# One block for projections, softmax and products of a triangular attention, in place of two

## Chip, cores, metric

One NeuronCore of a Trainium2 chip. The metric is the device time of one execution in microseconds (us); of several executions the median counts. [...]

## What is computed

The program computes two layers over x (2, 64, 64, 256). Only the first is touched by the change, and of it the attention:

```python
B, N, _, E = x_in.shape          # 2, 64, 64, 256
H = 8;  d_k = E // H             # 8 heads of 32
q, k, v1, v2 = (x_in @ W).reshape(B, N, N, H, d_k)   # W = Wq, Wk, Wv1, Wv2
scores = einsum('bilhd,bljhd->biljh', q, k) / sqrt(d_k)
att = softmax(scores, axis=2)    # over l
out = einsum('biljh,bilhd,bljhd->bijhd', att, v1, v2)
attn_out = out.reshape(B, N, N, E) @ Wo
```

Behind it come a residual, two layer norms and an MLP (`block_mlp`), and the second layer, a pair of Mamba scans (`block_mamba`). Neither is changed.

## The kernel before

The program is written out per engine: every engine has its own list of instructions in order, and semaphores (`wait_ge`, `then_inc`) tie the lists together. No scheduler decides an order. A DMA is issued in order by the queue of the engine on whose list it stands: nearly all by SP, some by POOL (GpSimd). PE is the matrix engine (TensorE), DVE VectorE, ACT ScalarE.

`block_projections` takes the 8192 tokens in 16 steps of 512 (`CHUNK`). Each step turns its x on PE (8 transposes), ACT copies the result out as `xT_hi` and DVE subtracts to make `xT_lo` (products use three terms of high and low parts, `SPLIT`), then come 24 matmuls for queries and keys (L208) and 24 for the two values (L218). ACT and DVE copy the results out (L273, L277), POOL's queue stores them to DRAM (`qk_dram` L179, `v_dram` L182).

`block_attention` starts when that block is over. Heads are taken in four pairs (`PAIRS`), n; the two batches stand beside each other. For one pair the work is:

- `scores(n, g)`, 16 groups g of 4 values of l: PE, out of `q` and a chunk `kb` of keys (8 values of l a chunk, two buffers, 4 DMAs a chunk, L359); `copy_scores` by ACT (L545) into `raw`.
- the softmax in 8 parts k of 8 values of j: `least` of the negated scores by DVE (L450), `exps` by ACT (16 instructions a part, each followed by the read of its accumulator, which is the row's sum, L555), `invert` by DVE (L455), `norm` by POOL (L434), `turn(n, g)` by PE (L506, two groups a part), `copy_att` into `att` (L459 by DVE, L562 by ACT).
- the products, 64 steps t of two rows i each: `av` = `att` times v2, 22 of 32 values of d by DVE and 10 by POOL (both L420), then for each row four small groups of matmuls with `w` (v1 spread out, `build` by ACT) on PE (`row`, L520), and `evict` by ACT (L592). `av` has two buffers (a product waits until the rows of the step before last are done), the results three PSUM banks. A store of 4 rows is 8 DMAs on SP's queue (L377).

A stage c is one pair and one batch, 32 steps; there are 8. Its v2 is loaded as `v2in` (values of d next to each other), and ACT turns it (`turn_v2`, 4 instructions, L569 and L573): DVE's part into PSUM, `v2ps`, POOL's into SBUF, `v2sb`. Both products of the stage's first step wait for that. It is done behind row 61 (`i == N - 3`) of the stage before:

```python
if c + 1 < NC and i == N - 3:
    turn_v2(c + 1)
```

For pair 0 scores and softmax stand by themselves, ahead of the first product. For pairs 1 to 3 they are strewn between the 64 product steps of the pair before: scores in steps 0 to 15, exps from step 18 on (`EXPS`), and the rest behind them by the tables `LEAST_AT`, `INVERT_AT`, `NORM_AT`, `TURN_AT`.

Of the kernel before, what the change touches and what calls it, by code (L numbers as in the profile page):

```python
# [112 lines left out]
def block_projections(nc, x, W, qk_dram, v_dram):  # L113

    STEPS = TOK // CHUNK
    with ExitStack() as ctx:
        t_ = Tools(nc, ctx, "prj")  # L120
        sb, sem = t_.sb, t_.sem
        bank = t_.banks()
        T_, Q_, V_ = bank[0:2], bank[2:6], bank[6:8]
        ident = sb("ident", [P, P])
        wqk = sb("wqk", [P, 2, KT, E])
        wv = sb("wv", [P, KT, 2, E])
        wqk_ = {n: sb(f"wqk_{n}", [P, 2, KT, E], F32R) for n in ("hi", "lo")}
        wv_ = {n: sb(f"wv_{n}", [P, KT, 2 * E], F32R) for n in ("hi", "lo")}
        xin = [sb(f"xin{u}", [P, TT, E]) for u in range(2)]
        xT = {n: [sb(f"xT{u}_{n}", [P, KT, CHUNK], F32R) for u in range(2)] for n in ("hi", "lo")}  # L130
        w_split = sem("w_split")
        qk = [sb(f"qk{u}", [P, 4, CHUNK]) for u in range(2)]
        vs = [sb(f"vs{u}", [P, TT, 2 * E]) for u in range(2)]
        ident_set, qk_w_loaded, v_w_loaded = sem("ident_set"), sem("qk_w_loaded"), sem("v_w_loaded")
        x_loaded = [sem(f"x_loaded{u}") for u in range(2)]
        transposed, xT_hi_ready, xT_lo_ready = sem("transposed"), sem("xT_hi_ready"), sem("xT_lo_ready")
        qk_done, qk_by_act, qk_by_dve = sem("qk_done"), sem("qk_by_act"), sem("qk_by_dve")
        v_done, v_by_act, v_by_dve = sem("v_done"), sem("v_by_act"), sem("v_by_dve")
        qk_stored = [sem(f"qk_stored{u}") for u in range(2)]
        v_stored = [sem(f"v_stored{u}") for u in range(2)]  # L140
        block = ctx.enter_context(nc.Block())
        rows = x.rearrange("(g t p) c -> g p t c", t=TT, p=P)
        qk_out = qk_dram.rearrange("(m p) t -> p m t", p=P)
        v_out = v_dram.rearrange("(g t p) c -> g p t c", t=TT, p=P)

        def stages(eng, step):

            step(0, 0, False)
            step(1, 1, False)
            with eng.Fori(1, STEPS // 2 - 1) as r:  # L150
                step(r * 2, 0, False)
                step(r * 2 + 1, 1, False)
            step(STEPS - 2, 0, False)
            step(STEPS - 1, 1, True)

        @block.sync
        def _(sp):
            def load(t, u):
                need(sp, transposed, 2 * t - 2)
                sp.dma_start(xin[u][:, :, :], rows[t]).then_inc(x_loaded[u], 16)  # L160

            load(0, 0)
            for m, name in enumerate(("Wq", "Wk")):
                sp.dma_start(wqk[:, m], W[name].rearrange("(k p) n -> p k n", p=P)).then_inc(qk_w_loaded, 16)
            load(1, 1)
            for m, name in enumerate(("Wv1", "Wv2")):
                sp.dma_start(wv[:, :, m], W[name].rearrange("(k p) n -> p k n", p=P)).then_inc(v_w_loaded, 16)
            with sp.Fori(1, STEPS // 2) as r:
                load(r * 2, 0)
                load(r * 2 + 1, 1)  # L170

        @block.gpsimd
        def _(pool):
            make_identity(pool, ident, ident_set)

            def store(t, u, last):
                pool.wait_ge(qk_by_act, 2 * t + 2)
                pool.wait_ge(qk_by_dve, 2 * t + 2)
                pool.dma_start(qk_out[:, :, bass.ds(t * CHUNK, CHUNK)], qk[u][:, :, :]).then_inc(qk_stored[u], 16)  # L179
                pool.wait_ge(v_by_act, 2 * t + 2)  # L180
# [1590 lines left out]
```

## Time and profile before

| | us |
|---|---|
| median of 3 executions (2548.08 to 2550.58) | 2548.24 |
| the profiled execution | 2545.53 |
| its span, first to last instruction | 2543.9 |
| projections, until the last matmul | 201 |
| scores and softmax of pair 0, until the first product | 109 |
| 256 product steps, until the next block | 868 |
| the two other blocks | 1365 |
| busy: PE 2121, DVE 1982, ACT 1340, POOL 1014 | |

The profile is of one execution on the one core. Busy time of an engine says little here, since the stages have different limits: read each stage by itself, and in it the wait that ends last. `SPq` and `POOLq` are rows of DMAs being issued, not of their transfers. Two instructions that follow each other overlap by some 0.1 us in the rows, so the distance of two starts is the price of one, not its length.

### The profile page before, as it was taken

How to read it: one execution, taken by the hardware profiler on the slowest of the kernel's cores; microseconds unless marked ns; L12 is line 12 of the kernel's file. 1: busy time of each engine (PE TensorE's matmuls, PEld its weight loads, DVE VectorE, ACT ScalarE, POOL GpSimd, SP SyncE). 2: the span in 40 equal slices, each digit the busy share in tenths (PEclk: the TensorE clock that was granted, in tenths of full speed). 3: DMA queues.
4: the chain of work that ended last, by engine and by line, in shares of the span. 5: the costliest groups of instructions: out<-in, count | busy, mean ns of one | idle time of the engine just before them, and what ended most of it. 6: DMA issues, size and time to landing. Idle time of an engine off the chain costs nothing. (4 is left out here: it accounts for less than half of the span.)

```text
span 2543.9 us, 42568 instructions
## 1 busy us (share of the span) xinstructions
PE 2121.4 (83%) x16504; PEld 1381.1 (54%) x16504; DVE 1982.1 (78%) x2320; ACT 1340.4 (53%) x2922; POOL 1014.4 (40%) x515
## 2 busy tenths in 40 slices
PE   8994386776678677664999996999999999999998
PEld 7883231232223121111677665777777777777776
DVE  3330598988998998996677775888888888888886
ACT  2222877866876885442233333555555545555552
POOL 1110388988998999995011001111111112111111
PEclk9997598999999999998999998999999999999999
DMA  5656324123212212113123215232222223333332
GB/s 191 222 214 145 62 43 75 20 47 72 36 25 54 43 20 35 20 19 86 53 94 94 87 55 108 60 82 75 68 67 68 71 77 97 86 92 95 89 76 59
DMA packets 322721, 195.96 MB, mean 77 GB/s; under 512 B 235232, under 2 KB 304352, under 8 KB 317920
## 3 DMA queue, kind: packets, MB, share of 16 engines
q1 hardware_dynamic: 313824, 159.78, 26.7%
q0 software_dynamic: 8704, 33.56, 3.4%
q8 instruction: 127, 2.08, 0.3%
q14 instruction: 66, 0.54, 0.1%
HBM read 125.37 MB, written 67.90 MB: 76 GB/s over the span
## 5 line engine op out<-in xcount | busy, mean ns | idle before, releaser
L420 DVE TENSOR_TENSOR att_av<-att_att,att_v2ps 128x2816 f32<-128x2816 f32 x256 | 773.4, 3077 | 64.3 <-PE att_bank L520 35.1
L420 POOL TENSOR_TENSOR att_av<-att_att,att_v2sb 128x1280 f32<-128x1280 f32 x256 | 745.9, 2932 | 81.0 <-PE att_bank L520 62.4
L520 PE MATMUL att_bank<-att_av,att_w 128*32 128x512 f32 x4096 | 538.9, 616 | 234.7 <-DVE att_av L420 214.0
L1586 DVE SCALAR_TENSOR_TENSOR mb_cv<-mb_bank,mb_cw,mb_cv 128x504 f32<-128x504 f32 (+2 forms) x480 | 343.1, 730 | 126.4 <-ACT mb_cv L1409 121.4
L520 PEld LDWEIGHTS att_bank<-att_av,att_w 128*32 128x32 f32 x4096 | 130.2, 111 | 568.1 <-issue 305.8
L592 ACT ACTIVATE att_ev<-att_bank 128x512 f32<-128x512 f32 x512 | 298.9, 596 | 236.7 <-PE att_bank L520 212.5
L1229 POOL TENSOR_TENSOR mb_rstd<-mb_ms,mb_neghalf 128x4 f32<-128x4 f32 x32 | 32.3, 1009 | 795.2 <-DVE mb_ms L1630 795.2
L1290 PE MATMUL mb_bank<-mb_xT_hi,dt_win_hi 128*128 128x512 f32 x576 | 241.7, 420 | 36.8 <-DVE mb_cv L1586 35.4
L1348 PE MATMUL mb_bank<-mb_wf,mb_y 128*128 128x256 f32 x1024 | 246.9, 389 | 0.9 <-DVE mb_y L1626 0.9
L1290 PE MATMUL mb_bank<-mb_xT_lo,dt_win_hi 128*128 128x512 f32 x576 | 229.2, 398 | 0.0
L1290 PE MATMUL mb_bank<-mb_xT_hi,dt_win_lo 128*128 128x512 f32 x576 | 228.7, 397 | 0.0
L1409 ACT ACTIVATE mb_cv<-mb_bank,mb_cw 128x512 f32<-128x512 f32 x160 | 110.5, 691 | 202.1 <-PE mb_bank L1290 197.9
L1348 PEld LDWEIGHTS mb_bank<-mb_wf,mb_y 128*128 128x128 f32 x1024 | 189.0, 192 | 51.1 <-issue 26.8
L555 ACT ACTIVATE att_raw<-att_raw,att_least 128x64 f32<-128x64 f32 x512 | 170.2, 338 | 2.1 <-DVE att_least L450 1.3
L1290 PEld LDWEIGHTS mb_bank<-mb_xT_hi,dt_win_hi 128*128 128x128 f32 x576 | 109.0, 189 | 89.1 <-DVE mb_cv L1586 61.9
L1595 DVE TENSOR_TENSOR_SCAN mb_S<-mb_dAb,mb_inj 128x512 f32<-128x512 f32 x128 | 152.5, 1212 | 0.0
L1222 POOL TENSOR_TENSOR mb_inj<-mb_diag,dt_dt 128x512 f32<-128x512 f32 x128 | 130.0, 1047 | 33.9 <-DVE mb_S L1595 33.8
L496 PE MATMUL att_x<-att_kb,att_q 64*64 64x128 f32 x1024 | 76.7, 295 | 58.3 <-DMA att_kb<-qk_t 57.7
L1290 PEld LDWEIGHTS mb_bank<-mb_xT_hi,dt_win_lo 128*128 128x128 f32 x576 | 109.1, 189 | 26.4
L1429 ACT ACTIVATE mb_xc<-mb_cv,mb_cb 128x512 f32<-128x512 f32 x128 | 91.9, 718 | 58.3 <-DVE mb_cv L1586 58.3
L496 PEld LDWEIGHTS att_x<-att_kb,att_q 64*64 64x64 f32 x1024 | 65.9, 194 | 103.3 <-DMA att_kb<-qk_t 51.1
L1290 PEld LDWEIGHTS mb_bank<-mb_xT_lo,dt_win_hi 128*128 128x128 f32 x576 | 109.3, 190 | 21.2
(170 smaller groups left out, 3395.6 us busy)
## 6 DMA issues: line engine op xcount, KB each, us to landing
qk_t<-prj_qk POOLq DMA_DIRECT2D x16, 1024.0 KB, 5.8
v<-prj_vs POOLq DMA_DIRECT2D x16, 1024.0 KB, 4.7
mixed_t<-att_ev SPq DMA_DIRECT2D x1024, 8.0 KB
mb_dAb<-dA_rows SPq DMA_DIRECT2D x32, 512.0 KB, 5.7
mb_dAb<-dA_cols SPq DMA_DIRECT2D x32, 512.0 KB, 6.0
prj_xin<-in_x SPq DMA_DIRECT2D x16, 512.0 KB, 3.7
att_q<-qk_t SPq DMA_DIRECT2D x8, 1024.0 KB, 9.9
att_kb<-qk_t SPq DMA_DIRECT2D x128, 64.0 KB, 2.2
```

Of the source, the lines that this page charges most:

```text
L420: eng.tensor_tensor(av[t % 2][:, :, d0:d1, :], a.unsqueeze(2).broadcast_to((P, 2, d1 - d0, N)), v2.unsqueeze(1).broadcast_to((P, 2, d1 - d ...
L496: mm = pe.matmul(X_[g % 2][r, l4 * P:(l4 + 1) * P], qv[r, g * LB + l4, :], kb[c % 2][r, (g * LB + l4) % KL, :, :], start=True, stop=True)
L520: mm = pe.matmul(bank[r % NB][s * M:(s + 1) * M, :], w[i // WB % 2][:, i % WB, s, :], av[r // 2 % 2][:, i % 2, s * STRIP_D:(s + 1) * STRIP ...
L555: ins = act.activation(raw[:, j, h, :], raw[:, j, h, :], ACT.Exp, scale=-1.0, bias=least[:, j, h:h + 1], accum_out=rsum[:, j, h:h + 1])
L592: act.activation(ev[e % 2][:, i % EB, :], bank[(c * N + i) % NB][:, :], ACT.Copy).then_inc(o_copied, 1)
L1222: pool.tensor_tensor(inj[:, p], diag[:, :].unsqueeze(1).broadcast_to((P, NH, L)), dtt[way(c)][:, c % NCHUNK * PAIR + p, :].unsqueeze(2).br ...
L1290: mm = pe.matmul(PR_[b][:, :], win_[w][:, k, col:col + P], xT_[x][:, k, :], start=(n == 0), stop=(n == 3 * KT - 1))
L1348: mm = pe.matmul(YA_[t // 2][:, (t % 2) * E:(t % 2 + 1) * E], y[:, m, t * P:(t + 1) * P], wf[way(c)][:, m, :], start=(m == 0), stop=(m == ...
L1409: act.activation(cv[:, m, :], PR_[j % 2][:, :], ACT.Copy, scale=cw[way(c)][:, m, TAPS - 1:TAPS])\
L1429: act.activation(xc[c % 2][:, m, :], cv[:, m, :], ACT.Silu, bias=cb[way(c)][:, m:m + 1]).then_inc(x_silued, 1)
L1586: dve.scalar_tensor_tensor(out=dst, in0=src, scalar=cw[way(c)][:, m, TAPS - 1 - back:TAPS - back], in1=dst, op0=ALU.mult, op1=ALU.add)\
L1595: dve.tensor_tensor_scan(S[:, p, :], dAb[:, p, :], inj[:, p].rearrange("p h t -> p (h t)"), 0.0, ALU.mult, ALU.add).then_inc(scanned, 1)
```

## The change

`block_projections` is gone; `block_attention` takes over its work in two passes over x.

- Pass 1, 16 steps t: queries and keys only (`project_qk`), six PSUM banks in turn.
- Pass 2, 16 steps v: x is loaded and turned a second time, values only (`project_v`, three banks). Pair 0 runs beside it: scores in v = 2 to 5 (four groups each), exps of part v-6 in v = 6 to 13, sums, `invert` and `norm` of part v-7 in v = 7 to 14, turning of part v-8 in v = 8 to 15. q, keys, v1 and v2 are loaded by SP between the loads of x.
- Sums of pair 0, and of parts 5 to 7 of the other pairs, are a `tensor_reduce` of DVE in place of ACT's accumulator (`SUMS_BY_ACT = 5`).
- The first two steps of every stage (`FRESH = 2`) multiply by `v2in` as it was loaded, in place of `v2ps` and `v2sb`; they wait for the load alone. `turn_v2` moves to the start of the stage's last step, and the load of the next v2 also waits for the two steps.
- `kb` has its two halves outermost, so that a key DMA writes 2 KB in one piece per partition, not 8 pieces of 256 B.
- In the products' stages SP issues the load of the next keys ahead of the store, not behind it. `EXPS` is a table with 0 or 1 value of j in steps 30 to 32.

The diff, cut to what is spoken of below:

```diff
+    XN = TOK // CHUNK
+    SUMS_BY_ACT = 5
+    FRESH = 2
...
-        kb = [sb(f"kb{u}", [P, KL, 2, N]) for u in range(2)]
+        kb = [sb(f"kb{u}", [P, 2, KL, N]) for u in range(2)]
...
+        SCORES_AT = {v: range(4 * (v - 2), 4 * (v - 1)) for v in range(2, 6)}
+        EXPS_BESIDE = {v: v - 6 for v in range(6, 14)}
+        SUM_BESIDE = {v: v - 7 for v in range(7, 15)}
+        TURN_BESIDE = {v: v - 8 for v in range(8, 16)}
...
+        PER_STEP = [0] * 18 + [2] * 12 + [1, 0, 1] + [2, 2, 1] * 8
+        EXPS = [(min(N, sum(PER_STEP[:m])), min(N, sum(PER_STEP[:m + 1]))) for m in range(STEPS)]
...
+            for u in range(2, XN + 2):
+                load_x(u)
             sp.wait_ge(kb_zeroed, 2)
+            for u in range(2):
+                sp.wait_ge(qk_stored[u], XN // 2 * 16)
             load_q(0)
             load_k(0, 0)
             load_k(0, 1)
+            load_x(XN + 2)
+            load_x(XN + 3)
...
+            load_x(XN + 7)
+            load_q(1)
+            load_k(1, 0)
+            load_k(1, 1)
+            for v in range(8, 11):
+                load_x(XN + v)
...
                     sp.wait_ge(v2_in_ps, c + 1)
+                    sp.wait_ge(av_by_dve, c * (N // 2) + FRESH)
+                    sp.wait_ge(av_by_pool, c * (N // 2) + FRESH)
                     load_v2(c + 1)
                 for e in range(N // EB):
+                    if c % 2 == 0 and n < PAIRS and e < N // KL - 2:
+                        load_k(n, e + 2)
                     store(c, e)
                     if c + 1 < NC and e in (7, 14):
                         sp.wait_ge(w_built, (c * 8 + (4 if e == 7 else 8)) * 2)
                         load_v1(c + 1, 0 if e == 7 else 1)
-                    if c % 2 == 0 and n < PAIRS and e < N // KL - 2:
...
             if m == 0:
+                eng.wait_ge(v2_loaded, c * 32 + 32)
+            if m == FRESH:
                 eng.wait_ge(v2_ready, c + 1)
+            if m < FRESH:
+                v2 = v2raw[:, d0:d1]
...
+            for v in range(XN):
+                if v in SUM_BESIDE:
+                    norm(0, SUM_BESIDE[v])
+                for e in range(2):
+                    pool.wait_ge(v_by[e], 2 * v + 2)
+                pool.dma_start(v_out[v], vs[v % 2][:, :, :]).then_inc(v_stored[v % 2], 16)
...
+                js = slice(k * JK, (k + 1) * JK)
                 dve.wait_ge(exped, n * NK + k + 1)
-                dve.reciprocal(rinv[:, k * JK:(k + 1) * JK, :], rsum[:, k * JK:(k + 1) * JK, :]).then_inc(inverted, 1)
+                if n == 0 or k >= SUMS_BY_ACT:
+                    dve.tensor_reduce(rsum[:, js, :], raw[:, js, :, :], AX_X, ALU.add).then_inc(summed, 1)
+                    dve.wait_ge(summed, k + 1 if n == 0 else NK + (n - 1) * (NK - SUMS_BY_ACT) + k - SUMS_BY_ACT + 1)
+                dve.reciprocal(rinv[:, js, :], rsum[:, js, :]).then_inc(inverted, 1)
...
+            for v in range(XN):
+                evict_v(v, 1)
+                xT_lo(XN + v + 1)
+                evict_v(v, 3)
+                if v == 5:
+                    least_of(0, 0)
+                    least_of(0, 1)
+                if v in EXPS_BESIDE and EXPS_BESIDE[v] + 2 < NK:
+                    least_of(0, EXPS_BESIDE[v] + 2)
+                if v in TURN_BESIDE:
+                    copy_att(0, 2 * TURN_BESIDE[v] + 1)
+                if v in SUM_BESIDE:
+                    invert(0, SUM_BESIDE[v])
             for t in range(PAIRS * STEPS):
...
+            for v in range(XN):
+                for tile in range(TT):
+                    project_v(v, tile)
+                    if v in SCORES_AT:
+                        scores(0, SCORES_AT[v][tile])
+                    if v in TURN_BESIDE and tile < 2:
+                        turn(0, 2 * TURN_BESIDE[v] + tile)
+                    if tile == 1:
+                        turn_x(XN + v + 1)
...
+            for v in range(XN):
+                evict_v(v, 0)
+                if v in SCORES_AT:
+                    for g in SCORES_AT[v][:2]:
+                        copy_scores(0, g)
+                if v in TURN_BESIDE:
+                    copy_att(0, 2 * TURN_BESIDE[v])
+                xT_hi(XN + v + 1)
+                if v in EXPS_BESIDE:
+                    exps(0, EXPS_BESIDE[v] * JK, EXPS_BESIDE[v] * JK + JK // 2)
+                evict_v(v, 2)
+                if v in SCORES_AT:
+                    for g in SCORES_AT[v][2:]:
+                        copy_scores(0, g)
+                if v in EXPS_BESIDE:
+                    exps(0, EXPS_BESIDE[v] * JK + JK // 2, EXPS_BESIDE[v] * JK + JK)
+            build(0, 0)
...
+                c = t // (N // 2)
+                if c + 1 < NC and t % (N // 2) == N // 2 - 1:
+                    turn_v2(c + 1)
```

Three places in the lists of instructions. First DVE (VectorE), around the sums and `invert` of pair 0. `att_raw` holds the scores and later the exps, `att_vs` the values on their way to DRAM, `att_x` the turned softmax. Before, with nothing else on the engine:

```order
L455 RECIPROCAL att_rinv<-att_rsum 128x16 [waits att_exped]
L459 COPY att_att<-att_x 128x4x128 [waits att_turned] x2
L455 RECIPROCAL att_rinv<-att_rsum 128x16 [waits att_exped]
L459 COPY att_att<-att_x 128x4x128 [waits att_turned] x2
L455 RECIPROCAL att_rinv<-att_rsum 128x16 [waits att_exped]
```

and with the change, one pass v of the values (v = 11):

```order
L419 COPY att_vs<-att_bank 128x512 [waits att_v_done,att_v_stored1]
L406 TENSOR_TENSOR att_xT_lo<-att_v2ps,att_xT_hi 128x512 [waits att_xT_hi_ready] x2
L419 COPY att_vs<-att_bank 128x512 [waits att_v_done]
L377 TENSOR_REDUCE att_least<-att_raw 128x16
L390 COPY att_att<-att_x 128x4x128 [waits att_turned]
L384 TENSOR_REDUCE att_rsum<-att_raw 128x16 [waits att_exped]
L386 RECIPROCAL att_rinv<-att_rsum 128x16 [waits att_summed]
```

The reciprocal on which `norm` waits now stands last in the pass, behind the copy of the pass's fourth value tile.

Second PE, one pass v of the values from v = 8 on. `att_x` takes the turned softmax, and here `att_v2ps` takes the turned x:

```order
L480 MATMUL att_x<-att_ident,att_raw 128x128 [waits att_t_copied,att_normed]
L480 MATMUL att_x<-att_ident,att_raw 128x128 x3
L534 MATMUL att_bank<-att_wv_hi,att_xT_hi 128x512 [waits att_v_by_act]
...
L480 MATMUL att_x<-att_ident,att_raw 128x128 [waits att_t_by_dve]
L480 MATMUL att_x<-att_ident,att_raw 128x128 x3
L508 MATMUL att_v2ps<-att_ident,att_xin 128x128 [waits att_xT_lo_ready,att_x_loaded0]
L508 MATMUL att_v2ps<-att_ident,att_xin 128x128 x7
L534 MATMUL att_bank<-att_wv_hi,att_xT_hi 128x512 [waits att_v_by_dve]
...
```

The turning waits for `norm` behind the first of four value tiles, and the other three stand behind it.

Third DVE at the start of the products: before

```order
L420 TENSOR_TENSOR att_av<-att_att,att_v2ps 128x2x1408 [waits att_v2_in_ps,att_t_copied]
L420 TENSOR_TENSOR att_av<-att_att,att_v2ps 128x2x1408
L420 TENSOR_TENSOR att_av<-att_att,att_v2ps 128x2x1408 [waits att_i_done] x16
L450 TENSOR_REDUCE att_least<-att_raw 128x16 [waits att_s_copied]
```

and now

```order
L339 TENSOR_TENSOR att_av<-att_att,att_v2in 128x2x1408 [waits att_t_copied,att_v2_loaded,att_v_done,att_t_by_dve]
L339 TENSOR_TENSOR att_av<-att_att,att_v2in 128x2x1408
L339 TENSOR_TENSOR att_av<-att_att,att_v2ps 128x2x1408 [waits att_i_done,att_v2_in_ps]
L339 TENSOR_TENSOR att_av<-att_att,att_v2ps 128x2x1408 [waits att_i_done] x15
L377 TENSOR_REDUCE att_least<-att_raw 128x16 [waits att_s_copied]
```

The wait for `v2ps` has moved two products down, and the two ahead of it read `v2in`. The other seven stages begin alike, and POOL's lists too.

## Rows read from the trace of the kernel before

**Rows 1.** Stretches: length; busy PE, PEld, DVE, ACT, POOL; PEclk; DMA; GB/s

```profile
0.00:201.20 201.20, 192.53 (x896) 160.01 (x896) 67.86 (x99) 57.09 (x97) 24.28 (x37) 1.00 0.57 209
261.40:310.50 49.10, 15.75 (x64) 12.55 (x64) 25.30 (x32) 47.10 (x262) 15.22 (x8) 0.54 0.27 54
310.50:1178.70 868.20, 615.65 (x5040) 197.96 (x5040) 801.06 (x305) 594.07 (x1528) 789.47 (x280) 0.97 0.21 39
```

**Rows 2.** Timeline, PE in the projections and the scores: start us, us, instructions

```profile
10.61 0.77 PE L208 MATMUL prj_bank<-prj_xT_hi,prj_wqk_hi 128*128 128x512 f32 x1 [4.21 <-DVE prj_xT_lo L240]
...
18.84 1.03 PE L198 MATMUL prj_bank<-prj_ident,prj_xin 128*128 128x128 f32 x8
...
200.65 0.39 PE L218 MATMUL prj_bank<-prj_wv_hi,prj_xT_lo 128*128 128x512 f32 x1
200.87 0.39 PE L218 MATMUL prj_bank<-prj_wv_lo,prj_xT_hi 128*128 128x512 f32 x1
...
248.31 2.08 PE L496 MATMUL att_x<-att_kb,att_q 64*64 64x128 f32 x32 [1.26 <-DMA att_kb<-qk_t]
```

**Rows 3.** Timeline, DVE in the softmax of pair 0

```profile
261.36 9.10 DVE L450 TENSOR_REDUCE att_least<-att_raw 128x16 f32<-128x1024 f32 x8 [59.37 <-ACT att_raw L545]
270.38 0.24 DVE L455 RECIPROCAL att_rinv<-att_rsum 128x16 f32<-128x16 f32 x1
```

**Rows 4.** Timeline, POOL: the norm of one part

```profile
270.71 1.90 POOL L434 TENSOR_TENSOR att_raw<-att_raw,att_rinv 128x1024 f32<-128x1024 f32 x1 [57.54 <-DVE att_rinv L455]
```

**Rows 5.** The page's DMA issues (us from issue to landing); timeline, SP's queue

```profile
qk_t<-prj_qk POOLq DMA_DIRECT2D x16, 1024.0 KB, 5.8
prj_xin<-in_x SPq DMA_DIRECT2D x16, 512.0 KB, 3.7
att_q<-qk_t SPq DMA_DIRECT2D x8, 1024.0 KB, 9.9
...
261.47 7.00 SPq L359 DMA_DIRECT2D att_kb<-qk_t  x8
```

**Rows 6.** Timeline, one change of stage: DVE and PE

```profile
535.66 6.08 DVE L420 TENSOR_TENSOR att_av<-att_att,att_v2ps 128x2816 f32<-128x2816 f32 x2 [4.78 <-ACT att_v2ps L573]
...
538.89 3.44 PE L520 MATMUL att_bank<-att_av,att_w 128*32 128x512 f32 x16 [5.48 <-DVE att_av L420]
...
542.40 6.09 DVE L420 TENSOR_TENSOR att_av<-att_att,att_v2ps 128x2816 f32<-128x2816 f32 x2 [0.65 <-PE att_bank L520]
...
543.36 1.92 PE L520 MATMUL att_bank<-att_av,att_w 128*32 128x512 f32 x16
```

**Rows 7.** Waits over the product steps: us in total, times, longest us

```profile
DVE att_av L420 <- PE att_bank L520: 35.1, 30, 5.5
DVE att_av L420 <- ACT att_v2ps L573: 29.2, 7, 4.8
```

**Rows 8.** Groups of instructions, shapes apart: busy us, mean ns of one, idle before

```profile
L420 POOL TENSOR_TENSOR att_av<-att_att,att_v2sb 128x1280 f32<-128x1280 f32 x256 | 745.9, 2932 | 81.0 <-PE att_bank L520 62.4
...
L573 ACT ACTIVATE att_v2ps<-att_v2in 128x512 f32<-128x512 f32 x14 | 14.1, 1042 | 0.0
...
L459 DVE COPY att_att<-att_x 128x512 f32<-128x512 f32 x16 | 14.8, 1000 | 1.7 <-PE att_x L506 1.7
L277 DVE COPY prj_vs<-prj_bank 128x512 f32<-128x512 f32 x32 | 22.1, 692 | 53.2 <-PE prj_bank L218 53.2
```

**Rows 9.** Timeline in the MLP's block: DVE beside POOL's two casts

```profile
1286.42 1.22 DVE L946 TENSOR_TENSOR mlp_h<-mlp_h,mlp_be 128x1024 f32<-128x1024 f32 x1
1286.94 3.80 POOL L742 CAST dt_win_hi<-mlp_win 128x1152 fp32r<-128x1152 f32 x2 [97.47 <-DMA mlp_win<-in_mh_in_wT]
1287.67 2.05 DVE L963 TENSOR_TENSOR mlp_hb<-mlp_h,mlp_b 128x1024 f32<-128x1024 f32 x1
```

**Rows 10.** Timeline, SP's queue in the steps with scores: one store, one chunk of keys

```profile
335.86 4.87 SPq L377 DMA_DIRECT2D mixed_t<-att_ev  x8
...
340.77 1.92 SPq L359 DMA_DIRECT2D att_kb<-qk_t  x4
```

More of the change, by code:

```diff
@@ L296, in block_attention @@
     STEPS = N
+    XN = TOK // CHUNK
+    SUMS_BY_ACT = 5
+    FRESH = 2
+    TERMS = [(k, xn, wn) for k in range(KT) for xn, wn in SPLIT]
     with ExitStack() as ctx:
@@ L386, in _ @@
                 load_v1(0, half)
[L387 to L391 removed]
+            for v in range(11, XN):
+                load_x(XN + v)
+            for u in range(2):
+                sp.wait_ge(v_stored[u], XN // 2 * 16)
             for c in range(NC):
@@ new lines, in evict_v @@
+            def evict_v(v, tile):
+                if tile == 1:
+                    need(dve, v_stored[v % 2], v // 2 * 16)
+                dve.wait_ge(v_done, TT * v + tile + 1)
+                dve.tensor_copy(vs[v % 2][:, tile, :], bank[(TT * v + tile) % NB][:, :]).then_inc(v_by[1], 1)
+            split_w(0)
+            xT_lo(0)
+            for t in range(XN):
+                evict_qk(t, 1)
+                xT_lo(t + 1)
+                evict_qk(t, 3)
+                if t == 1:
+                    split_w(1)
@@ new lines, in project_v @@
+            def project_v(v, tile):
+                r = TT * v + tile - NB
+                if tile == 0:
+                    pe.wait_ge(xT_lo_ready, 2 * (XN + v) + 2)
+                if v == 0:
+                    pe.wait_ge(w_split, 4)
+                    for e in range(2):
+                        pe.wait_ge(qk_by[e], 2 * XN)
+                if r >= 0:
+                    pe.wait_ge(v_by[r % 2], r // 2 + 1)
+                for i, (k, xn, wn) in enumerate(TERMS):
+                    mm = pe.matmul(bank[(TT * v + tile) % NB][:, :], xT[xn][v % 2][:, k, tile * P:(tile + 1) * P],
+                                   wv_[wn][:, k, :], start=(i == 0), stop=(i == len(TERMS) - 1))
+                mm.then_inc(v_done, 1)
@@ new lines, in _ @@
+            turn_x(0)
+            pe.wait_ge(w_split, 2)
+            for t in range(XN):
+                project_qk(t, 0)
+                project_qk(t, 1)
+                turn_x(t + 1)
+                project_qk(t, 2)
+                project_qk(t, 3)
+            for v in range(XN):
+                for tile in range(TT):
+                    project_v(v, tile)
[3 more added lines that the diff above has]
+                        turn(0, 2 * TURN_BESIDE[v] + tile)
+                    if tile == 1:
+                        turn_x(XN + v + 1)
@@ L528, in _ @@
             for t in range(PAIRS * STEPS):
                 n, m = t // STEPS + 1, t % STEPS
+                if t == 0:
+                    for e in range(2):
+                        pe.wait_ge(v_by[e], 2 * XN)
                 for i in (0, 1):
@@ L561, in copy_att @@
                 act.wait_ge(turned, n * (N // JB) + g + 1)
+                if n == 1 and g == 0:
+                    for u in range(2):
+                        act.wait_ge(v_stored[u], XN // 2 * 16)
                 act.activation(att[n % 2][:, :, g * JB:(g + 1) * JB].rearrange("p m j -> p j m"),
@@ L596, in evict, with xT_hi @@
                     build(c + 1, 0)
-                if c + 1 < NC and i == N - 3:
-                    turn_v2(c + 1)
-            for g in range(NG):
-                copy_scores(0, g)
-            exps(0, 0, N)
+            def xT_hi(u):
+                if u < 2 * XN:
+                    if 2 <= u < XN + 2:
+                        act.wait_ge(qk_done, 4 * (u - 1))
+                    elif u >= XN + 2:
+                        act.wait_ge(v_done, TT * (u - XN - 1))
+                    for k in range(KT):
+                        act.wait_ge(transposed, 2 * u + k + 1)
+                        act.activation(xT["hi"][u % 2][:, k, :], T_[u // XN][k], ACT.Copy).then_inc(xT_hi_ready, 1)
```

326 lines of the change are left out of this document (140 added, 186 removed).

## Prediction, made before the changed kernel was run

> **What bounds the kernel now.** I read the table of stretches first [rows 1]. In the projections PE is busy 193 of 201 us at full clock: PE is the bound. In the softmax of pair 0 PE has 15.8 us of work in 49 and clock 0.54, DVE 25 us, ACT 47: nothing overlaps much, and from 201.2 to 310.5 the kernel spends 109 us on what the change wants to hide. In the product steps DVE is busy 801 of 868 us: DVE is the bound, and its idle time is the loss. The waits [rows 7] name that: 29.2 us for `v2ps` at the seven changes of stage, 35.1 us for PE. The 1365 us behind 1178.7 are untouched and only shift.
>
> The sum is made against the profiled execution, 2545.5 us; the median of the runs shown is 2.7 us above it, and I add that at the end. About 0.2% (5 us) is what a measurement of this kernel tells from no change.
>
> **Pass 1.** A step before is (200.87 + 0.23 - 10.61) / 16 = 11.9 us. Matmuls follow each other at 200.87 - 200.65 = 0.227 us, so 24 are 5.45, and the eight transposes 1.0 [rows 2]. A pass is 6.45 us. Sixteen, with the slow first microseconds kept: 190.5 - 16 x 5.45 + 1.0 (one more turning) = 104.3, and PE is through at T1 = 114.9. ACT and DVE have two copies and two halves of the split each, under 3 us: hidden.
>
> **Pass 2, v = 0 to 7.** v = 0: 0.9 (last copies) + 6.45, to 122.3. In v = 1 PE wants the x of v = 2 after two tiles, at 125.0. SP has that load behind the wait for the last store of keys (T1 + 0.9 + 5.8 = 121.6) and behind both loads of q, 9.9 us [rows 5]. It lands at about 134.5 (121.6 + 9.9 + 2 to 3.7). PE stands 9.5 us; then 3.7 us of work, and 1.5 because PE's clock has fallen (price below): 139.7. v = 2 to 5 carry four groups of scores, 32 matmuls in 2.08 us or 1.04 a group [rows 2]: 10.6 each, to 182.1. v = 6: 188.6. v = 7 meets the same pattern: x of v = 8 stands behind q and 8 key DMAs of pair 1, and those keys alone take 7.0 us to issue [rows 5]; by q's 9.9 it lands near 194.0, 2.7 late. v = 7 ends at 197.7. The exps take ACT some 4 us a pass and are hidden.
>
> **Pass 2, v = 8 to 15.** Here I see a loop that no engine's busy time shows. The turning in pass v waits for `norm`; that for `invert`; that stands at the end of DVE's pass, behind the copy of tile 4; and tiles 2 to 4 stand behind the turning on PE. Round the loop: turning 0.5, tile 1.36, turning 0.5, turning of x 1.0, two tiles 2.7, in all 6.2 with the gaps on PE [rows 2]; then on DVE latency 0.15, copy 0.65 [rows 8], least 1.13 (the start distance of eight in 9.10), copy of the softmax 0.95 (1.0 less the overlap) [rows 8], sum as a `tensor_reduce` of the same form 1.2, reciprocal 0.25 [rows 3], together 4.4; then norm 1.95 [rows 4]. That is 12.55 us where PE has 7.6 of work. [...] So 14.05 with the least, 12.9 without. v = 8 has no copy of the softmax ahead: 13.1. To the end: 197.7 + 13.1 + 4 x 14.05 + 3 x 12.9 = 305.7; the last copies, 1.7, and the first product starts at 307.4, not 310.5 [rows 1]. **Term 1: -3.** Ends: -29 (no late x, no clock lost: 9.5 + 2.7 + 1.5 + 12 less) and +8 (the doubled rate of stores and loads slows pass 1 by 0.5 a step).
>
> **The two fresh steps.** Before, a change of stage costs DVE 4.78 and then 0.65 us [rows 6]; all seven 29.2 and 5.2, 34.4 together. Now DVE starts at once, but two things are new in its product. It reads `v2in` 128 B apart. No DVE row shows such a read. Ends: 3.08 us as now (6.08 for two, less the overlap), and 5.3, by ACT's 1042 ns for 512 elements of this very tile against some 600 for plain ones. The nearest row of DVE is the copy that writes with a stride, 1000 against 692 ns [rows 8]: factor 1.45, which I take: 4.45. And both inputs now lie in SBUF, while POOL's product, 2.93 us, reads SBUF too. The MLP shows what that does: a DVE instruction with two SBUF inputs takes 2.05 us beside POOL's cast, where the same form takes 1.22 [rows 9]. The cast had begun 0.73 before it; it looks as if each waits for the other to end. So I take DVE and POOL in turn: DVE 4.45, POOL 2.93, DVE 4.45, POOL 2.93 = 14.8, rows on PE 1.4, and DVE's fourth product starts at 16.2 where undisturbed it would at 9.1: 7.1 late. In the middle of a pair a norm of POOL falls between: 9.0. **Term 2:** 4 x 7.1 + 3 x 9.0 - 34.4 = **+21**. The stage that begins all of it paid only 0.6 before: **+6.5**. Ends together: -35 (no cost at all) and +40 (5.3 us).
>
> [...]
>
> **Sums on DVE.** Three `tensor_reduce` in each of three pairs, 9 x 1.13 = **+10** on the bounding engine. ACT's saved accumulator reads are worth nothing while it waits for PE. Ends: 0, should DVE happen to be waiting, and +11.
>
> **Keys ahead of the store.** In the 16 steps with scores DVE waits on PE, and PE on keys. Of the 35.1 us [rows 7], 18 lie there (6.1, 6.3 and 5.7 in the three pairs); 2 are clock after a change of stage. Keys now leave about 5 us earlier, by one store of 4.87. SP still needs 4.87 + 1.92 = 6.8 us for a store and a load [rows 10] against 6.0 for two steps, so its lateness grows to 4 us by the last chunk, which about eats the slack: **-14**, ends 0 and -16.
>
> **The queue of q.** Two of the 30 waits [rows 7], one of them the longest, 5.5 us, the other 4.8, stand behind the issue of the next pair's q and 8 key DMAs. In pieces of 2 KB these move faster: **-4**, ends 0 and -10. The new `EXPS` table moves a few exps by a step: 0, covered by ACT's idle time; without that cover a step would be late by one exp.
>
> **Sum:** -3 + 21 + 6.5 + 10 - 14 - 4 = +16.5, so 2562 on the profiled execution and **2565** as a median.
>
> **Rivals.**
> 1. DVE and POOL don't block each other. For it: the row is of a cast, not of a product [rows 9]. Against: the 0.83 us lost are just what was left of the cast. A stage then starts 2 x 1.4 late by the stride alone: 20 - 34 = -14, the start +2.3, total 2526; without a price for the stride either, 2502. Faster. Chance 0.16.
> 2. The loop beside the values is shorter: the clock holds, x is in time. It turns the sign once v = 8 to 15 take under 12 us each and x is less than 3 us late. Term 1 becomes -29: 2539, faster. For it: PE works 7.6 of 13 us there, and the scores behind a gap of 1.26 us ran at full clock [rows 2]. Against: my gaps are of 4 to 5 us, and one of 5.48 lost the clock [rows 6]. Chance 0.19.
> 3. They block each other, but the stride is free: 4.3 and 6.2 us a stage, 36 - 34 = +2, start +4: 2544. No change. Chance 0.13. This is also the case in which the change doesn't do what it says: the wait for `v2ps` is gone and a wait for the other engine has its place.
> 4. POOL's product slows as well on the new reads, by the same 1.45: 2 x 1.3 more in each of eight stages, +21: 2586. Chance 0.10. [...]
>
> **The numbers.** My own case has 0.42, and by itself ranges from 2548 to 2586. Faster by over 0.2%: rival 1 whole, most of rival 2 (0.15), a part of 3 (0.05), a little of my own: 0.37. Within: 0.10, from 3, 2 and mine. Slower: 0.53. The range goes from 2510 to 2588: below it lies only rival 1 at its far end, above it a part of rival 4 and my own upper bounds together.
>
> **What would show it.** First product at 307 us, not 285; in v = 8 to 15 PE idle before the turning, released by POOL's norm, and starts of that turning 13 to 14 us apart. At each change of stage no wait for `v2ps`, but two DVE products longer than 3.1 us, the second one by POOL's 2.9, and POOL's two likewise; the fourth product 7 to 9 us late. Nine sums back to back with products. No wait of PE for keys but in the last chunks. Wrong I would be if DVE's products of `v2in` take 3.1 us side by side with POOL's, or if the values' passes take 8 us each.

## The result, and the profile after

The changed kernel takes 2621.15 us (median of 4, 2618.71 to 2627.98) against 2549.14 us: ratio 1.029, 95% interval 1.0272 to 1.0307. **Slower** by 72 us; the prediction was 2565, with a range to 2588. The profiled execution took 2628.0 us, 7 above the median, with a span of 2626.2, 82.3 us above the span before.

The stretches of the changed kernel: first pass, second pass with pair 0's softmax, product steps (columns as in [rows 1]).

```profile
0.00:115.70 115.70, 105.36 (x520) 87.99 (x520) 47.59 (x70) 38.91 (x67) 15.77 (x25) 1.00 0.67 227
115.70:326.40 210.70, 150.28 (x824) 119.95 (x824) 68.81 (x96) 92.19 (x218) 27.18 (x25) 0.85 0.52 158
326.40:1264.70 938.30, 632.03 (x5040) 198.39 (x5040) 883.19 (x313) 575.45 (x1387) 874.39 (x281) 0.93 0.19 37
```

The first product starts at 326.4, not 310.5: +15.9. The product steps take 938.3, not 868.2: +70.1. What follows them is 3.7 us shorter. DVE's busy time in the product steps rose by 82 us (883 against 801). An instruction that is held up while it runs counts as busy too (a fresh product of DVE shows 7554 ns here, and 5092 in e3, without a product of POOL beside it), so the groups have to say what it is.

At what, the groups say (busy us, mean ns of one, idle before), with shapes apart:

```profile
L339 DVE TENSOR_TENSOR att_av<-att_att,att_v2in 128x2816 f32<-128x2816 f32 x16 | 120.2, 7554 | 0.0
L339 POOL TENSOR_TENSOR att_av<-att_att,att_v2in 128x1280 f32<-128x1280 f32 x16 | 94.5, 5919 | 0.2
```

Sixteen fresh products of DVE take 120.2 us; at 3.0 us each they would take 48. That is +72 by itself. One change of stage, DVE and POOL, then PE:

```profile
569.73 11.86 POOL L339 TENSOR_TENSOR att_av<-att_att,att_v2in 128x1280 f32<-128x1280 f32 x2
570.13 16.48 DVE L339 TENSOR_TENSOR att_av<-att_att,att_v2in 128x2816 f32<-128x2816 f32 x2
```

```profile
578.32 3.52 PE L494 MATMUL att_bank<-att_av,att_w 128*32 128x512 f32 x16 [6.04 <-DVE att_av L339]
...
586.75 3.64 PE L494 MATMUL att_bank<-att_av,att_w 128*32 128x512 f32 x16 [3.81 <-DVE att_av L339]
```

POOL begins first, by 0.4 us; then DVE and POOL end in turn, DVE's second one 16.5 us after the start of its first. The rows on PE that follow each run at the lower clock (granted 0.50 from 578.5 to 581.5 and from 587.0 to 590.0), 3.5 to 3.6 us for 16 matmuls in place of 1.92. DVE's fourth product starts at 590.45, that is 20.3 us after the first. Undisturbed it would be 9.1 us, so it is 11.2 us late.

In the first stage DVE goes first, and its two products take 3.3 us less; in the second a norm of POOL waits for a DVE product as well:

```profile
326.38 13.22 DVE L339 TENSOR_TENSOR att_av<-att_att,att_v2in 128x2816 f32<-128x2816 f32 x2
...
453.02 6.62 POOL L353 TENSOR_TENSOR att_raw<-att_raw,att_rinv 128x1024 f32<-128x1024 f32 x1
```

The waits of ACT, DVE and PE that changed most: us in total, times, longest. Before, in the product steps, ACT waited 23.2 us for stores and PE 19.1 for keys.

```profile
ACT att_ev L630 <- DMA mixed_t<-att_ev: 73.4, 28, 8.3
...
DVE att_av L339 <- PE att_bank L494: 52.6, 34, 5.9
...
PE att_x L470 <- DMA att_kb<-qk_t: 0.2, 1, 0.2
```

The `v2ps` wait of 29.2 us [rows 7] is gone. The wait for PE has grown from 35.1 to 52.6: 20.0 of it stands right behind the eight fresh pairs. PE no longer waits for keys, but ACT waits three times as long for its stores.

The second pass, at its two late x loads and in its loop (start us, us, and the wait ahead):

```profile
139.07 1.97 PE L508 MATMUL att_v2ps<-att_ident,att_xin 128*128 128x128 f32 x8 [13.83 <-DMA att_xin<-in_x]
211.29 1.97 PE L508 MATMUL att_v2ps<-att_ident,att_xin 128*128 128x128 f32 x8 [10.38 <-DMA att_xin<-in_x]
```

```profile
258.86 1.21 DVE L377 TENSOR_REDUCE att_least<-att_raw 128x16 f32<-128x1024 f32 x1
259.98 1.01 DVE L390 COPY att_att<-att_x 128x512 f32<-128x512 f32 x1
...
260.84 1.19 DVE L384 TENSOR_REDUCE att_rsum<-att_raw 128x16 f32<-128x1024 f32 x1
262.07 0.25 DVE L386 RECIPROCAL att_rinv<-att_rsum 128x16 f32<-128x16 f32 x1
262.41 1.89 POOL L353 TENSOR_TENSOR att_raw<-att_raw,att_rinv 128x1024 f32<-128x1024 f32 x1 [11.20 <-DVE att_rinv L386]
...
264.36 1.12 PE L480 MATMUL att_x<-att_ident,att_raw 128*128 128x128 f32 x4 [4.79 <-POOL att_raw L353]
...
267.98 0.69 DVE L419 COPY att_vs<-att_bank 128x512 f32<-128x512 f32 x1 [5.66 <-PE att_bank L534]
```

This is the loop that the prediction drew: DVE's reciprocal, POOL's norm, PE's turning behind it, PE's tiles, and DVE's eviction, which waited 5.7 us. The first evictions of these steps stand at 226.3, 240.4, 254.2, 268.0, 281.7, 293.8, 307.2 and 321.1.

### The profile page after: what moved, and what is told of

Its sections match the earlier page's. It is cut to its first block and busy times, and to the rows that moved or that the text cites. A ratio compares the mean times of both kernels' runs of the same rounds, so it can differ in the third digit from the quotient of the medians.

```text
span 2626.2 us, 42406 instructions
## 1 busy us (share of the span) xinstructions
PE 2162.6 (82%) x16632; PEld 1397.0 (53%) x16632; DVE 2087.7 (79%) x2361; ACT 1332.6 (51%) x2690; POOL 1098.6 (42%) x513
## 5 line engine op out<-in xcount | busy, mean ns | idle before, releaser
L494 PE MATMUL att_bank<-att_av,att_w 128*32 128x512 f32 x4096 | 553.2, 640 | 308.0 <-DVE att_av L339 265.1
L339 DVE TENSOR_TENSOR att_av<-att_att,att_v2ps 128x2816 f32<-128x2816 f32 x240 | 725.7, 3076 | 52.6 <-PE att_bank L494 52.6
L339 POOL TENSOR_TENSOR att_av<-att_att,att_v2sb 128x1280 f32<-128x1280 f32 x240 | 716.9, 3003 | 62.9 <-PE att_bank L494 59.2
L1369 PEld LDWEIGHTS mb_bank<-mb_xT_hi,dt_win_hi 128*128 128x128 f32 x576 | 109.1, 189 | 88.8 <-DVE mb_cv L1665 61.7
L353 POOL TENSOR_TENSOR att_raw<-att_raw,att_rinv 128x1024 f32<-128x1024 f32 x32 | 80.1, 2503 | 96.4 <-DVE att_rinv L386 96.4
L339 DVE TENSOR_TENSOR att_av<-att_att,att_v2in 128x2816 f32<-128x2816 f32 x16 | 120.2, 7554 | 0.0
L891 PE MATMUL mlp_bank<-mlp_hT,mlp_w 128*128 128x512 f32 x256 | 117.8, 598 | 0.0
```

The costliest lines, as they stand in the source:

```text
L339: eng.tensor_tensor(av[t % 2][:, :, d0:d1, :], a.unsqueeze(2).broadcast_to((P, 2, d1 - d0, N)), v2.unsqueeze(1).broadcast_to((P, 2, d1 - d ...
L494: mm = pe.matmul(bank[r % NB][s * M:(s + 1) * M, :], w[i // WB % 2][:, i % WB, s, :], av[r // 2 % 2][:, i % 2, s * STRIP_D:(s + 1) * STRIP ...
L891: mm = pe.matmul(HID_[m][:, :], w1[:, k, m * P:(m + 1) * P], hT[u][:, k, :], start=(k == 0), stop=(k == KT - 1))
L1369: mm = pe.matmul(PR_[b][:, :], win_[w][:, k, col:col + P], xT_[x][:, k, :], start=(n == 0), stop=(n == 3 * KT - 1))
```

## The experiments

Twelve kernels. Unless said otherwise, each is the changed kernel with one edit. Each was timed in turn with the kernel before on the same chip (2547 to 2548 us on each of the four chips used), so ratios to that kernel are compared. For place, from each profile: when the first product starts (P), and how long it is from there to DVE's first instruction of the next block (S).

| | median us | ratio (95%) | P | S |
|---|---|---|---|---|
| before | 2549.1 | 1 | 310.5 | 891.3 |
| changed | 2621.2 | 1.029 (1.0272 to 1.0307) | 326.4 | 960.0 |
| e1 no fresh | 2568.1 | 1.0084 (1.0067 to 1.0101) | 323.0 | 898.3 |
| e2 no stride | 2582.8 | 1.0131 (1.0114 to 1.0148) | 322.3 | 918.3 |
| e3 POOL's part away | 2575.7 | 1.0106 (1.009 to 1.0123) | 322.5 | 909.4 |
| e4 reciprocal first | 2583.6 | 1.0148 (1.0119 to 1.0178) | 287.2 | 956.8 |
| e5 sums by ACT | 2615.3 | 1.0267 (1.0253 to 1.0281) | 320.2 | 948.4 |
| e6 store first | 2623.0 | 1.0296 (1.0282 to 1.031) | 325.2 | 956.1 |
| e7 keys split | 2608.1 | 1.0228 (1.021 to 1.0247) | 319.2 | 943.3 |
| e8 x early | 2607.4 | 1.024 (1.0226 to 1.0254) | 307.1 | 959.5 |
| e9 no fresh, old turn | 2563.9 | 1.0074 (1.006 to 1.0088) | 324.3 | 890.6 |
| e10 all but the split | 2498.1 | 0.9804 (0.9791 to 0.9818) | 263.7 | 892.2 |
| e11 e10 + split | 2479.9 | 0.9736 (0.9723 to 0.975) | 262.5 | 872.7 |
| e12 before + split | 2527.5 | 0.9915 (0.9902 to 0.9929) | 308.4 | 876.4 |

P differs by up to 7 us between kernels that are alike up to there (319 to 326), so 326.4 is at the high end; and the profiled execution of the changed kernel was the slowest of its four. P and S are of one execution each: a difference of a few us between them shows nothing.

### e1: no fresh products

```
-    FRESH = 2
+    FRESH = 0
-                    sp.wait_ge(av_by_dve, c * (N // 2) + FRESH)
-                    sp.wait_ge(av_by_pool, c * (N // 2) + FRESH)
```

> No fresh products: all 20 pairs of a stage read v2ps and v2sb, as before the change, and SP does not wait for the two pairs before it loads the next v2. Theory (the strided read of v2in, in turns with GpSimd's, costs the extra time of the product stages): the 16 DVE products of 7554 ns become 3.1 us ones, the following waits on PE go, the v2ps wait of 4.8 us at seven changes comes back; 57.5 us less than the changed kernel's, about 2564 us. Rival (the extra time of the product stages has another source, such as the stores that now land late behind the keys): under 20 us less, 2601 us or more. Rival (the prediction's own sum for the pairs): 27.5 us less, about 2594 us.

53 us less, S 61.7 less. Over two thirds of the loss of 72 us is in the fresh pairs, net of the wait for `v2ps` that comes back without them.

### e2 and e3: what the fresh products are made of

e2 reads as many elements without the stride (so they are not the right ones). In e3 POOL only writes zeros in its share of the fresh products and reads nothing:

```
-                v2 = v2raw[:, d0:d1]
+                v2 = v2in[:, :, :].rearrange("p j d -> p (j d)")[:, d0 * N:d1 * N].rearrange("p (d j) -> p d j", j=N)
```

```
+            if m < FRESH and d0 > 0:
+                eng.memset(av[t % 2][:, :, d0:d1, :], 0.0).then_inc(ready, 1)
+                return
```

> The fresh products of both engines read v2in's bytes in order, without the stride (the products of these pairs are then of the wrong elements: d and j are mixed; the work is the same in size). Theory (VectorE and GpSimd take turns at SBUF in these pairs, and each also pays for the stride): without the stride DVE's own part falls from 4.85 to 3.1 us and GpSimd's from 3.5 to 2.9, the two still in turns, so DVE's mean falls from 7554 to about 6000 ns, and 16 of them with their waits give 25 to 30 us less than the changed kernel, about 2594 us. Rival (no turns, the stride alone is what the 7.5 us are): mean 3.1 us and about 57 us less. Rival (turns alone, the stride free): mean stays near 7.5 and the time at 2621 us.

> GpSimd writes zeros in place of its share (d 11 to 15) of the fresh products, from no input (those elements of the product are then zero). Theory (turns plus stride): DVE's fresh product is left with its own part and so falls from a mean of 7554 ns to about 4.85 us, and the time by 16 x 2.7 = 43 us and some of the waits, to about 2575 us. Rival (the stride is free for DVE, and all of its extra is GpSimd's turn): mean 3.1 us, 2560 us or less. Rival (no turns: DVE's stride alone): mean stays at 7.5 us and the time at 2621 us.

DVE's and POOL's fresh groups in e2:

```profile
L339 DVE TENSOR_TENSOR att_av<-att_att,att_v2in 128x2816 f32<-128x2816 f32 x16 | 82.0, 5163 | 0.0
L339 POOL TENSOR_TENSOR att_av<-att_att,att_v2in 128x1280 f32<-128x1280 f32 x16 | 71.4, 4470 | 0.3 <-PE att_bank L494 0.2
```

and DVE's in e3:

```profile
L342 DVE TENSOR_TENSOR att_av<-att_att,att_v2in 128x2816 f32<-128x2816 f32 x16 | 80.7, 5092 | 0.0
```

Without a POOL product beside it, the strided product takes 5.09 us: that is the stride alone, 2.0 over the 3.08 of `v2ps`, with hardly any spread (4.995 to 5.278). Without the stride but with POOL's products beside, the mean is 5.16 and the shortest 3.09: that is the turns alone, 2.1. Both together, 7.55. So both costs are real and about equal, and a rival that has only one of them does not stand. e2 came 11 us lower than expected (5.16 us a product, not 6.0); e3 is as expected.

### e4: the reciprocal at the start of the step

```
             for v in range(XN):
+                if v in SUM_BESIDE:
+                    invert(0, SUM_BESIDE[v])
                 evict_v(v, 1)
...
-                if v in SUM_BESIDE:
-                    invert(0, SUM_BESIDE[v])
```

> In the value steps beside pair 0's softmax DVE's reciprocal for GpSimd's norm is moved from the end of its step to the start of the next one's beginning, ahead of the eviction of values, one block of norm earlier in DVE's order. Theory (steps 8 to 15 of about 13.7 us are a loop: reciprocal, norm on GpSimd, its transposes on PE, the evictions, and round to the reciprocal at the step's end): the loop is cut, a step falls to DVE's and PE's own work of 8 to 10 us, and the first product of v2 comes 8 x 4 to 8 x 5 us earlier, so 2580 to 2590 us. Rival (the steps are bound by DVE's own work beside GpSimd's norm, which still blocks it): steps stay at 13 to 14 us and the time at 2621 us.

P is 39 us earlier, the time 37.5 us less. The starts of the first eviction of four steps in e4, with what they waited:

```profile
216.01 0.69 DVE L419 COPY att_vs<-att_bank 128x512 f32<-128x512 f32 x1 [2.85 <-PE att_bank L534]
...
223.28 0.69 DVE L419 COPY att_vs<-att_bank 128x512 f32<-128x512 f32 x1 [1.23 <-PE att_bank L534]
...
230.54 0.69 DVE L419 COPY att_vs<-att_bank 128x512 f32<-128x512 f32 x1 [1.21 <-PE att_bank L534]
...
250.09 0.69 DVE L419 COPY att_vs<-att_bank 128x512 f32<-128x512 f32 x1 [2.90 <-PE att_bank L534]
```

7.3 us a step in place of 13.7, about PE's own 7.6 us of work in a step: the loop was the bound. The step of 19.6 us is the next limit: its x stands on SP's queue behind the loads of v2 and v1 (15.7 us of issuing), and DVE waits 10.5 us there.

### e5: all sums by ACT

```
-    SUMS_BY_ACT = 5
+    SUMS_BY_ACT = 8
```

> All eight sums of the softmax of pairs 1 to 3 are again written by ScalarE beside its exponentials (SUMS_BY_ACT = 8), as before the change; pair 0's stay on DVE. Theory (nine sums of 1.21 us stand on DVE's path in the product stages): 9 x 1.13 = 10 us less than the changed kernel, about 2611 us. Rival (they lie in DVE's waits for PE, or ScalarE's 192 exponentials of 0.33 instead of 0.25 us cost what they give): 0 to 3 us less, 2618 to 2621 us.

6 us less in the median, where 10 was expected; the intervals of the two ratios overlap. S is 11.6 less, which would fit the 10, but see e10: there the same edit shortens S by nothing. What the sums cost is not settled.

### e6: stores first again

```
-                    if c % 2 == 0 and n < PAIRS and e < N // KL - 2:
-                        load_k(n, e + 2)
                     store(c, e)
...
+                    if c % 2 == 0 and n < PAIRS and e < N // KL - 2:
+                        load_k(n, e + 2)
```

> SP's order in the product stages is again that of before: a stage's store first, then the two v1 loads, then the next keys. Theory (the keys ahead of the store take DVE's wait for the score steps away but hold up the store, so that ScalarE's wait for a store, 23.2 us before and 73.4 us after, stands in its place on the chain): ScalarE's wait falls by some 15 us, DVE's for PE rises by as much, and the time stays within 5 us of 2621 us. Rival (the store's wait is the price and the keys were never late): 10 us or more less. Second rival (the prediction's: the order is worth 14 us): 14 us more, about 2635 us.

No difference in the time. ACT's wait for stores and PE's for keys swap places:

```profile
PE att_x L470 <- DMA att_kb<-qk_t: 18.4, 16, 2.8
...
ACT att_ev L630 <- DMA mixed_t<-att_ev: 15.7, 5, 5.8
```

In this kernel the order of SP's queue only said who waits: PE for keys 18.4 us where it was 0.2, ACT for stores 15.7 where it was 73.4. The prediction's 14 us for it are refuted.

### e7 and e12: SP's issuing shared with ACT

```
-                        load_k(n, e + 2)
+                        load_k(n, e + 2, (0,))
...
                     copy_scores(n, m)
+                    if m % 2 == 1 and m // 2 + 2 < N // KL:
+                        load_k1(n, m // 2 + 2)
```

`load_k1` issues the two key DMAs of batch 1 on ACT; SP's `load_k` keeps batch 0. e12 is the same edit in the kernel before.

> In the stages that compute scores, the key DMAs of one batch (2 of a chunk's 4, chunks 2 to 7) are issued by ScalarE, behind its copy of the scores that frees the buffer, and no longer by SP. Theory (in these stages SP's issuing is the bound: 4.87 us for a store and 1.83 for four key DMAs are 6.7 us back to back, against 6.09 us of two of DVE's products; in whichever order they stand, the 0.7 us of each two steps stay): SP needs 5.8 us, ScalarE 5.8, the waits of 0.7 us in the steps with scores go and ScalarE's wait for a store (73.4 us) falls to some 20; 12 to 16 us less than the changed kernel, about 2607 us. Rival (the waits come from PE's own work with scores, or ScalarE is then late itself): within 4 us of 2621 us.

> The kernel of before the change, with the key DMAs of one batch (chunks 2 to 7) issued by ScalarE instead of SP, as in e7; stores and keys in their old order. Theory (SP's issuing bounds the steps with scores before the change too, and the prediction's 14 us for a new order stood on a wrong reading of whose lateness it was): the waits of 0.7 us in each two steps with scores, 18 us in all three pairs, go; 12 to 18 us less than the kernel before, 2530 to 2535 us. Rival (before the change the keys were only in the wrong place, and the issuing did not bind): within 5 us of the kernel before.

SP's queue in the changed kernel, then in e7 (start us, us of issuing):

```profile
357.34 1.83 SPq L240 DMA_DIRECT2D att_kb<-qk_t  x4
359.22 4.88 SPq L258 DMA_DIRECT2D mixed_t<-att_ev  x8
364.14 1.83 SPq L240 DMA_DIRECT2D att_kb<-qk_t  x4
366.01 4.87 SPq L258 DMA_DIRECT2D mixed_t<-att_ev  x8
```

```profile
360.56 4.87 SPq L258 DMA_DIRECT2D mixed_t<-att_ev  x8
365.47 0.91 SPq L240 DMA_DIRECT2D att_kb<-qk_t  x2
366.43 4.87 SPq L258 DMA_DIRECT2D mixed_t<-att_ev  x8
371.34 0.90 SPq L240 DMA_DIRECT2D att_kb<-qk_t  x2
```

In the changed kernel SP issues without a pause, 6.8 us for what DVE does in 6.09, and DVE stands 0.7 us in each two steps. In e7 SP needs 5.9 us for its part, and between 355 and 440 us DVE waits for PE once instead of six times, 3.4 us instead of 11.2. e7 is 13 us faster than the changed kernel. e12 is 20.6 us faster than the kernel before, more than the 12 to 18 expected (S 14.9 less, P 2.1); DVE's wait for PE falls from 35.1 to 21.4 us. ACT's wait for stores in e7 falls to 42.4, not to the 20 expected.

### e8: x earlier

```
-            for u in range(2, XN + 2):
+            for u in range(2, XN + 3):
                 load_x(u)
...
-            load_x(XN + 2)
...
+            load_x(XN + 8)
             load_q(1)
```

> Two of SP's x loads of the second pass are issued earlier: x(18) before SP waits for the stores of the first pass and issues q and keys of pair 0; x(24) before q and keys of pair 1. Theory (the wait of 14.9 us on xT_lo in step 1 and the 10.4 us wait on x(24) in step 7 are SP's queue, and steps 2 to 5 would absorb little of it): the first product comes 15 to 20 us earlier and the time is 2601 to 2606 us. Rival (what is gained before step 8 is lost in the loop of steps 8 to 15, which runs by its own period, or q and keys are then late by as much): under 5 us, 2616 us or more.

14 us less, just short of the 15 to 20 expected, P at 307.1. PE's waits of 13.8 and 10.4 us for x are gone; there remain 1.0 for x and 5.8 for q ahead of the first scores, which PE now reaches sooner: they start at 135.7, not 146.9, with q issued at 120.7 and 121.0. The loop of steps 8 to 15 does not take the gain back.

### e9: old place of ACT's copy

e1, with `turn_v2(c + 1)` back behind row 61.

> No fresh products (as in e1) and ScalarE's copy of the next v2 again behind row 61, as before. Theory (what was left of the v2 wait in e1, 33 us in eight changes, is the same as before the change, 29 us): the same as e1 within 4 us, 2564 to 2572 us. Rival (the copy at the end of a pair's rows costs more than the old place, where it stands three rows earlier): 8 us or more less than e1, under 2560 us.

4 us less than e1, but the intervals overlap; these runs do not show that the place matters.

### e10 and e11: the parts together

e9, e4, e5 and e8 in one kernel. SP's first v2 load moves behind `load_x(XN + 11)`, the two v1 halves behind `load_x(XN + 12)` and `load_x(XN + 13)`. e11 adds e7's split.

> One kernel of the parts that the runs so far found to help: no fresh products, ScalarE's copy of the next v2 behind row 61, the reciprocal first in its step, x loads early (and v2's and v1's first loads spread between x loads of steps 11 to 14), all sums of pairs 1 to 3 by ScalarE. Theory (the prices add, since they lie in stages that follow each other): 2621 - 53 (e1) - 37.5 (e4) - 14 (e8) - 6 (e5), less up to 5 more for the x of step 11: 2505 to 2512 us, faster than the kernel before the change by 35 to 42 us. Rival (without its other limits the loop of steps 8 to 15 hits ScalarE's or the v stores' time and takes back what x gives): 2518 us or more.

> e10 with the key DMAs of one batch issued by ScalarE, as in e7. Theory (SP's issuing is the bound in the steps with scores): 12 to 16 us less than e10, about 2493 us. Rival: within 4 us of e10.

The parts add, with some to spare: e10 is 7 us below the expectation. What e10 gains on e9 is all in P: 60.6 us earlier, where e4 and e8 gave 39.2 and 19.3. S is 892.2, against 890.6 in e9, so that taking the sums off DVE brought nothing here: its busy time in the product steps falls by 10 us and its waits ahead of products rise by 13. Why, no run shows. e11 is 18 us faster than e10, where 12 to 16 were expected. e11's second pass, 115.7 to 262.5, in the columns of the stretches:

```profile
115.70:262.50 146.80, 132.67 (x821) 107.22 (x819) 68.45 (x95) 93.15 (x220) 29.40 (x26) 0.96 0.74 226
```

PE is busy 133 of 147 us at clock 0.96: PE is the bound again, as in the old projections. e11 is 2.6% faster than the kernel before the change and 5.4% faster than the changed one (from the two ratios). Against e12, which has the split too but the old two blocks, e11 is 48 us faster, and P is 46 us earlier: the block in one was worth having, once its loop was cut and its x in time. The fresh reads were not.

## Why the prediction was wrong

The sign was right, the size was not: +72 us in the medians where it had +16.5. Three terms failed: the late x loads and the fresh products were priced too low, and the order of SP's queue gave nothing. Its terms one by one, against the profile, which has +82.

**First product: -3 predicted, +15.9 measured** (some +12 by the median of the seven kernels with the same second pass). The loop of steps 8 to 15 was right to a microsecond: 109.7 us from the end of step 7 to the first product, 108.9 measured (217.5 to 326.4), and e4 shows that it is a loop. The 1.5 us that the sum adds behind a gap of PE ("price below") are the difference of two rows, 3.44 and 1.92 us [rows 6], at a granted clock of 0.50 (539 to 542) and 1.00 (543.36 to 545.28). The changed kernel shows as much: behind the gap of 4.79 us the granted clock was 0.50 from 264.36 to 266.5, and a turning and six matmuls took 3.35 us, where the same took an estimated 1.8 by their distances later in that step (0.44 for the turning, 0.227 for a matmul). What failed is the step "x of v = 8 ... lands near 194.0, 2.7 late". SP's queue (start us, us of issuing):

```profile
191.67 1.09 SPq L230 DMA_DIRECT2D att_q<-qk_t  x2
192.81 4.11 SPq L240 DMA_DIRECT2D att_kb<-qk_t  x8
196.96 16.70 SPq L225 DMA_DIRECT2D att_xin<-in_x  x3
```

The x was issued at 197.0, behind the keys, and PE could use it at 211.3 only. From the start of q's issue to that use it is 19.6 us, where the prediction had 11.9, q's 9.9 and 2 more. The first late x shows the same: 18.1 us (121.0 to 139.1), where it had 12.9. The prediction let x land 2 to 3.7 us behind q. In the trace both x were issued some 5 us behind it and then took 12.9 and 14.3 us to come into use. e8, which issues the two x loads ahead of q and keys, has no such waits; whether q's 2 MB, the keys or the stores of values at that time held the transfer up, no run tells apart. So PE stood 13.8 us for the first late x, not 9.5, and 10.4 for the second, not 2.7, and steps 2 to 5 took 11.6 us each, not 10.6. By the end of step 7 that makes 19.8 us. e8 gets 14 back by moving two loads.

**Fresh products, Term 2: +27.5 predicted with the start, +57 measured** (+71.6 of longer products, +20.0 of waits behind them, -34.4 of old waits). The mechanism held: DVE and POOL in turn, the stride on top. Three sizes were off. DVE's strided product: 4.45 taken; 4.97 at its shortest, 5.09 in e3, and an estimate of 4.85 where POOL's turns are taken off in the timeline. POOL's: 2.93 taken as unchanged, 3.52 at its shortest. And the order: the prediction let DVE go first; in seven of the eight stages POOL began first, and where no norm stands between, DVE then sits through POOL's turn twice. That is 10.7 to 11.2 us late at the four changes without a norm, where 7.1 stood, and 12.5 to 12.6 at the three with one, where 9.0 stood: 82 in all, less the 34.4, and 9.6 at the start. Of the rise of 4.1 at a change without a norm the two prices make about half (two DVE products at 0.4 to 0.5 more and two of POOL at 0.6), by this estimate; the rest is the order, which is read from the timeline and was not tested by a run of its own.

**Sums: +10 predicted.** DVE's nine sums take 10.9 us in the product steps. e5 gets 6 us back in the median and 11.6 in S, e10 against e9 nothing in S: the size stays open.

**Keys ahead of the store, -14, and the queue of q, -4: nothing measured in the changed kernel.** Without the fresh pairs' 20.0, DVE's wait for PE is 32.6 us, as against 35.1 less the 2 to 5 that went with the changes of stage. (In e1 and e9, without fresh pairs, it is 30.1 and 27.8, so 5 to 7 us less than before; no run says by what.) This step's own numbers held the answer: "SP still needs 4.87 + 1.92 = 6.8 us for a store and a load [rows 10] against 6.0 for two steps". That is most of the wait, and it is the same sum in either order. e6 shows the order worth nothing (2623.0 us against 2621.2), e7 and e12 show the issuing worth 13 to 21 us. The pieces of 2 KB landed no sooner (2.1 us against 2.2). Behind q they are issued faster, 3.9 us for eight against 7.0, but in the steps with scores four take 1.83 us against 1.92.

**The rivals.** Rival 1 (no turns) and rival 3 (stride free) are refuted by e2 and e3. Rival 2 (a shorter loop) too. Rival 4, POOL's read slower, was true in kind. It priced it at 1.3 us a product and 2586 in all; the trace has 0.6. The range ended at 2588 because no case in it was wrong in several terms at once; three terms missed by 19, 30 and 18 us, all on one side. That all three fell on the same side is chance, as far as the runs show.

DVE and POOL in turn stood on one cast before [rows 9]. The traces now show it for products, e2's 5.16 us in the mean beside POOL and 3.09 at the shortest, and for the norm, 6.62 us beside a strided product of DVE and 1.90 without one. POOL's product went from 2.88 to 3.52 us at its shortest, 22% more, with one of its two inputs strided, where the prediction's factor for rival 4 was 1.45.

## What to carry to other kernels

- Reading an operand where the DMA put it saves a copy only if the reader takes it at the copy's price. Here a 4.8 us wait was traded for two DVE products at 7.6 instead of 3.1 us: the copy in PSUM both packed the elements and kept DVE out of GpSimd's turn (3.08 and 2.93 us side by side, against 5.16 and 4.47 with v2 packed in SBUF, e2).
- Where work is laid beside other work, draw the loop of semaphores through one step and sum it, on all engines. The loop was 13.7 us where the busiest engine had 7.6, and one line moved ahead in DVE's order halved it. Then look for the next late thing, in the issuing queue of the loads.
- Where SP's queue issued without a pause, 6.8 us for each 6.09 of DVE, its order was worth nothing (e6); count its microseconds of issuing per step against the period, and give some of it to an engine that has time.

## What the runs showed of the hardware that was not expected

- A DVE product of 128x2816 f32 with one input read 128 B apart took 5.09 us (e3) against 3.08 with that input packed in PSUM, and 3.09 at its shortest packed in SBUF (e2).
- GpSimd's norm (both inputs in SBUF, 1.90 us alone) took 6.62 us beside a strided DVE product, at 453.0 us of the changed kernel, and 11.66 us beside two of them, at 696.2. That is 4.7 and 9.8 us more than alone, about one and two of DVE's strided products (4.97 us at the shortest).
- An x load of 512 KB, issued 5 us behind q's two DMAs of 1 MB and behind eight of keys, came into use 14.3 us after its issue (197.0 to 211.3); the median of x loads is 4.4 us from issue to landing.
